# Attention scores in float32 halves: the second pass of the two wide pieces as two 64-row matmuls

## The reference, cut to what matters

```
q, k, v = heads of the projected sources          # (8, 1250, 64) each
logits  = einsum('hqd,hkd->hqk', q * 64 ** -0.5, k)   # (one of four: causal mask)
att     = softmax(logits, axis=-1)
o       = einsum('hqk,hkd->hqd', att, v)
```

## Time and profile before

| | us |
|---|---|
| median of 3 runs | 3742.52 (3737.97 to 3744.35) |
| the profiled execution | 3732.09 |
| its span, first to last instruction | 3730.3 |
| PE busy in it | 2981.9 (80%) |
| DVE busy | 2136.2 (57%) |
| ACT busy | 1615.4 (43%) |
| POOL busy | 999.5 (27%) |
| mean granted TensorE clock | 0.909 of 2.4 GHz |

### The profile page before, as it was taken

The page is one execution under the profiler, slowest core; times in us unless marked ns, Lnnn a source line. Parts: engine busy times, 40 slices in busy tenths (PEclk is TensorE's granted clock), DMA queues, the critical chain, the costliest instruction groups (busy, mean ns, idle before and its releaser), DMA issues. The chain is left out here.

```text
span 3730.3 us, 46536 instructions
## 1 busy us (share of the span) xinstructions
PE 2981.9 (80%) x16234; PEld 2303.2 (62%) x16234; DVE 2136.2 (57%) x3599; ACT 1615.4 (43%) x3503; POOL 999.5 (27%) x965
## 2 busy tenths in 40 slices
PE   0405858999849977799999387878999899998798
PEld 0201227788646754477777376668888787886676
DVE  6105763788631116577776436763688647886433
ACT  0100013677414534444444235652677536774422
POOL 4777746465014422333331000000000000001110
PEclk9757989999959998899999589999999999999899
DMA  3105755442148974544431255213422043311322
GB/s 101 33 6 158 210 163 165 95 78 42 35 148 269 343 257 125 201 129 125 121 110 43 85 175 136 58 48 117 125 52 62 8 143 102 73 38 38 87 75 78
DMA packets 232673, 415.62 MB, mean 111 GB/s; under 512 B 48865, under 2 KB 146447, under 8 KB 228347
## 3 DMA queue, kind: packets, MB, share of 16 engines
q1 hardware_dynamic: 175787, 276.17, 25.0%
q0 software_dynamic: 56208, 136.40, 13.5%
q10 hardware_dynamic: 448, 0.08, 0.0%
HBM read 320.88 MB, written 95.47 MB: 112 GB/s over the span
## 5 line engine op out<-in xcount | busy, mean ns | idle before, releaser
L849 DVE TENSOR_TENSOR at_s<-at_pb,at_s 125x500 fp32r<-125x500 f32 (+1 forms) x864 | 482.0, 584 | 190.4 <-ACT at_s L762 190.0
L762 ACT ACTIVATE at_s<-at_pb 125x500 fp32r<-125x500 f32 (+1 forms) x864 | 447.8, 519 | 271.7 <-PE at_pb L679 269.1
L679 PE MATMUL at_pb<-ident,at_p 125*125 125x125 f32 x2880 | 477.3, 280 | 32.5 <-ACT at_p L777 14.3
L679 PEld LDWEIGHTS at_pb<-ident,at_p 125*125 125x125 f32 x2880 | 417.1, 190 | 128.7 <-DVE at_s L849 71.5
L696 PE MATMUL at_pb<-at_s,at_v 125*128 125x250 f32 x2880 | 483.4, 296 | 7.5 <-DVE t_t L861 3.9
L839 DVE TENSOR_REDUCE at_max<-at_pb 125x1 f32<-125x1250 f32 (+4 forms) x320 | 423.0, 1322 | 12.2 <-PE at_pb L664 7.6
L777 ACT ACTIVATE at_p<-at_pb,at_max 125x1250 f32<-125x1250 f32 (+4 forms) x320 | 382.7, 1196 | 29.7 <-DVE at_max L839 28.3
L696 PEld LDWEIGHTS at_pb<-at_s,at_v 125*128 125x128 f32 x2880 | 383.2, 191 | 14.1 <-DVE at_s L849 7.2
L1289 PE MATMUL so_ps<-g_got,g_hot 128*125 128x512 f32 x332 | 178.9, 642 | 201.7 <-DMA g_got<-support,g_edges 170.1
L2023 ACT ACTIVATE g_hot<-g_plain,g_edges 128x125 f32<-128x125 f32 x704 | 223.1, 388 | 253.4 <-PE g_pm L2007 239.8
L1970 POOL DMA_INDIRECT g_got<-nodes,g_edges x176 | 166.5, 946 | 388.2 <-DVE g_msg L2053 269.4
(11 more groups left out here) (293 smaller groups left out, 5377.1 us busy)
## 6 DMA issues: line engine op xcount, KB each, us to landing
w_ring<-in_L_ffn_w SPq DMA_DIRECT2D x128, 512.0 KB, 11.2
at_shared<-k_parts SPq DMA_DIRECT2D x64, 312.5 KB
ml_w<-in_mlp_w SPq DMA_DIRECT2D x64, 256.0 KB
k_parts<-at_shared SPq DMA_DIRECT2D x64, 250.0 KB, 3.0
q_parts<-at_shared SPq DMA_DIRECT2D x64, 250.0 KB, 3.1
h_edges<-em_both SPq DMA_DIRECT2D x11, 1024.0 KB, 4.4
g_h<-h_edges SPq DMA_DIRECT2D x11, 1024.0 KB, 6.4
at_shared<-q_parts SPq DMA_DIRECT2D x32, 312.5 KB
```

Of the source, the lines that this page charges most:

```text
L679: ins = pe.transpose(pturn[0:TN, g % 2, TN * (t % 4):TN * (t % 4) + TN], p[:, u % 2, TN * t:TN * t + TN], c.ident[0:TN, 0:TN])
L762: act.activation(p_hi[:, u // 2 % 2, 4 * n:4 * n + m, TN * (u % 2):TN * (u % 2) + TN], pturn[0:TN, g % 2, 0:TN * m].rearrange("p (a b) -> ...
L849: dve.tensor_tensor(p_lo[at], pturn[0:TN, g % 2, 0:TN * m].rearrange("p (a b) -> p a b", b=TN), p_hi[at].bitcast(F32), ALU.subtract).then_ ...
```

## The change

For a unit with more than one piece, the first pass of the first and of the second piece stay as they are. Their second passes move behind the first pass of the second piece and run over 64 rows each: one on the rows of the head's own half, where `q_two` has the high part of q, the other on the other half. For that one a new tensor `q_swap` holds the high part of q of each head on the opposite half; it takes 625 columns a tensor, so two of them for each pair buffer, one of the two for the second buffer lying in free columns of `shared`. `load_pair` has four more loads a pair, of 64 rows by 625, and `LOADS` goes from 12 to 16. In these two pieces the product of the low parts of q and k is no longer part of the sum. The third piece, and a unit's only piece, keep both passes over 128 rows. ACT and DVE are unchanged.

```diff
+        HN = N // 2
+        q_swap = [[sb(f"at_qs{n}", [128, HN], F32R) for n in range(2)], [None, sb("at_qs2", [128, HN], F32R)]]
...
+        q_swap = [[t[:, :] for t in q_swap[0]], [shared[:, 6 * N:6 * N + HN], q_swap[1][1][:, :]]]
...
-        LOADS = 12
+        LOADS = 16
...
                 for h, r in enumerate((top, low)):
                     eng.dma_start(q_two[j % 2][h][r, :].bitcast(F32), q_d[0, j, r, :]).then_inc(sem, 16)
                     eng.dma_start(q_two[j % 2][h][(low, top)[h], :].bitcast(F32), q_d[1, j, r, :]).then_inc(sem, 16)
+                    for n in range(2):
+                        eng.dma_start(q_swap[j % 2][n][(low, top)[h], :].bitcast(F32), q_d[0, j, r, HN * n:HN * n + HN])                            .then_inc(sem, 16)
...
                     a, b = there[n]
+                    q_at = slice(TN * i, TN * i + TN)
...
-                    pe.matmul(score[u % 2][0:TN, a:b], q_two[j % 2][h][:, TN * i:TN * i + TN], k_hi[j % 2][h][:, a:b],
+                    paired = len(there) > 1 and n < 2
+                    pe.matmul(score[u % 2][0:TN, a:b], q_two[j % 2][h][:, q_at], k_hi[j % 2][h][:, a:b],
                               start=True, stop=False)
-                    ins = pe.matmul(score[u % 2][0:TN, a:b], q_two[j % 2][h][:, TN * i:TN * i + TN], k_lo[j % 2][h][:, a:b],
-                                    start=False, stop=True)
+                    if not paired:
+                        ins = pe.matmul(score[u % 2][0:TN, a:b], q_two[j % 2][h][:, q_at], k_lo[j % 2][h][:, a:b],
+                                        start=False, stop=True)
+                    elif n == 1:
+                        for (a, b), q, r in ((there[0], q_two[j % 2][h], h), (there[1], q_swap[j % 2][i // (NT // 2)], 1 - h)):
+                            at = q_at if r == h else slice(TN * (i % (NT // 2)), TN * (i % (NT // 2)) + TN)
+                            r = slice(64 * r, 64 * r + 64)
+                            ins = pe.matmul(score[u % 2][0:TN, a:b], q[r, at], k_lo[j % 2][h][r, a:b],
+                                            start=False, stop=True)
```

## The result

The changed kernel takes 3750.72 us, the kernel before 3735.62 (medians of 20 runs each): ratio 1.0037, 95% interval 1.0028 to 1.0046, so 15 us slower where 23 us less were forecast.

The account below looks back on a forecast made before the run. It took a ring of waits through all engines as the bound, PE's order holding one of two units and DVE the other. Terms -27, -2 and +6 gave -23 us, from 3742.5 to 3720 us; range 3712 to 3750.

Parts of the forecast that it names:

- 1, the moved pass: Loops without mask: first piece's second pass moved behind second piece's first pass saves 0.23 us per two units, -27 us.
- T1: PE's second group of transposes, four of them, of the unit two before; forecast to start 0.23 us earlier.
- 2, the tiles: Second passes of the two wide pieces as two 64-row tiles; claimed to cost 0, even without overlap.
- p: Time from the start of the two second passes to T2; taken at or under 0.57 us, gain gone at 0.80.
- B1: First pass of the second wide score piece, 512 columns, on PE; the second passes were to follow it.
- T2: PE's third group of transposes, two of them, of the unit two before; forecast within 0.57 us of the tiles' start.
- C: The third score piece, 226 columns, on PE; p up to 0.49 us was to cost it nothing.
- 3, the causal loop: Loop with the causal mask: 3.5 us gained, 1.5 lost in short odd units; net -2 us, bounds -4 and +2.
- A granted clock under 0.95: Sign in the loops of the changed profile that would show the forecast wrong; no term of it covered this.
- 4, the loads: Four more q loads per pair of heads delay each loop's start 1.5 us; four loops, +6 us, bounds 2 and 10.
- partly eaten: Rival: p between 0.57 and 0.75 us leaves half the moved pass's gain, -14 us; 3732 us; chance 0.2.
- The slower rival: Rival: tiles run one after the other and each switch empties the array, p = 1.04; +28 us, 3774 us; chance 0.12.

## Why the prediction was wrong

The forecast and the result differ by 38 us. Read from the profiled executions they are some 17 in the loops without mask, 17 in the causal one, 5 in the starts.

- *1, the moved pass, -27 us:* right, and shown alone: the three loops are 29 us shorter with the tiles left out, and T1 starts 0.31 behind A1.
- *2, the tiles, "I take p at or under 0.57": cost 0.* This step failed. The size of p was as I took it: the tiles start 0.32 after B1 and T2 0.42 after them, in the prediction's measure p = 0.74 - 0.24 = 0.50. The cost was not 0, because the limits were incomplete. I asked when C and L786 would be late (0.49 and 0.57) and not when the copy of T2 would, which follows directly on the exponential: T2 may end 0.04 before 2752.96, that is at 2752.92, and with its 0.48 start at 2752.44, 0.63 after B1. That is p = 0.39. It is over by 0.11, in every second step, and the copy of T2, then L800 and L863, the addition and the reduce stand behind it: 117 x 0.11 = 13 us, with which -27 becomes -14; -10 was measured. Of the 0.11, 0.10 is T2 itself: I had left it its 0.38, with which the limit would be 0.49, and weights not loaded ahead made it 0.48. The earlier trace rows had that 0.48 already, at 2727.64, for a T2 whose weights were not loaded ahead.
- *The Trainium skill's drain rule* ("TensorEngine Tiling (Array Packing)", Key Properties) agrees with the traces in part: behind each change of rows the next weights are not loaded ahead, and it costs 0.08 before the tiles, 0.19 behind them (0.10 of it the tiles' own weights) and 0.10 in T2, some 0.37 a unit against the 0.24 saved. But the next matmul still starts 0.07 before the row ahead of it ends; the full tails that I had made of the rule (0.81) do not show. The rule on row groups in "TensorE: Matmul & The Clock Gate", Part 3, agrees too: the two start within 0.01 us of each other and last as long as one.
- *3, the causal loop, -2 us:* wrong in sign, +14.7, as large an error as the one before. The gain that it counts, 3.5 us, is there with the order alone, 3.2. The term that failed is the up to 0.1 us for a second pass behind the wait: it held no switch. In short units both switches stand between two waits, and nothing covers them: four 250-key units go from 9.0 to 9.8 us at full clock, and the four groups of 500 keys from 44.4 to 53.9 us together, at a lower clock. "A granted clock under 0.95, which none of my terms holds" is what came there, 0.86; how much of the 14.7 is the clock's stays open.
- *4, the loads, +6 us, bounds 2 and 10:* right in mechanism, too small, 11.4 to 12. The middle of the bounds was taken where the bytes set it, which was the upper bound's argument (2.6 a loop; 2.8 measured in the last three with the loads alone).
- The rivals: "partly eaten" is what happened in the loops without mask, but at p = 0.50, under the 0.57 where it begins, and by another follower than the one named. The slower rival put its place at L786 with p over 0.80; the slow-down came from two places that it did not name. The forecast that even without overlap p = 0.47 costs nothing holds for 128-row passes (298 us) and not for 64-row ones (312 us).
- A slip: the lower end of the range should be 3742.5 - 27 - 4 + 2 = 3713.5 us, not 3712.

## What to carry to other kernels

When an instruction is made longer ahead of a sync point, list every reader of what follows it, each with its own slack; the one left out here had the least. Here a pair of matmuls on both array halves saved 0.24 us and the two switches around it cost 0.37; by these numbers, an estimate that no run tests, two pairs or more would have to stand between two switches. Try the reordering that such a change needs first and by itself, since here it was the whole gain. A term that is small in long units has to be priced again in the shortest ones, where nothing covers it.

## What the runs showed of the hardware

- Two 64-row matmuls of 512 columns on different row halves last 0.49 us together, one after the other on the same half 0.72.
- Going from 128 to 64 rows and back costs some 0.37 us at the 2.4 GHz level: each time 0.08 or 0.09 more from one matmul to the next, and 0.10 for weights that are not loaded ahead. Between two 64-row matmuls on the same half the weights are loaded ahead, by 0.23 us.
- Four more loads of 64 rows by 625 columns in front of a wait made a start 2.8 us longer, four of 64 by 16 at most 0.6, which is within the scatter (one run).
